# Perceiver block on one core: key and value tiles interleaved, the attention loop's side work in another order

## The reference

```python
x = x + xattn(layernorm(x), ctx, ctx)   # 32 query heads, 8 key and value heads, head size 128, rope, causal
x = x + attn(layernorm(x))              # 32 heads of size 16, biases, causal
x = x + ffn(layernorm(x))               # base product + 8 experts of rank 16, gated by softmax - threshold
```

## Time and profile before

| | |
|---|---|
| profiled execution, its time | 786.1 us |
| its span, first to last instruction | 784.3 us |
| median of three runs | 786.59 us |
| PE busy | 724.8 us (92%) |
| DVE, ACT, POOL busy | 522.3, 376.0, 495.8 us |
| mean granted TensorE clock | 0.983 of full speed |
| DMA | 51.09 MB, mean 65 GB/s |
| chain that ended last | PE 55%, DVE 14%, POOL 12%, issue 11%, ACT 4% |

### The profile page before, as it was taken

The page is one execution under the profiler, slowest core; times in us unless marked ns, Lnnn a source line. Parts: engine busy times, 40 slices in busy tenths (PEclk is TensorE's granted clock), DMA queues, the critical chain, the costliest instruction groups (busy, mean ns, idle before and its releaser), DMA issues.

```text
span 784.3 us, 12899 instructions
## 1 busy us (share of the span) xinstructions
PE 724.8 (92%) x4848; PEld 566.7 (72%) x4848; DVE 522.3 (67%) x826; ACT 376.0 (48%) x555; POOL 495.8 (63%) x371
## 2 busy tenths in 40 slices
PE   8979995789999999999999999996999999999898
PEld 6758884667776786776777777775787777777786
DVE  4663545875676766846947847746567878888855
ACT  5455535535454444544643743543235676664220
POOL 4995307856677678676866866846323798975350
PEclk9999999989999999999999999997999999999999
DMA  8343461031121211302201201201100110011002
GB/s 330 108 161 122 121 187 54 1 122 38 58 68 41 81 39 40 107 13 66 81 29 51 94 27 54 95 3 60 48 0 1 42 39 18 1 36 48 14 1 107
DMA packets 25561, 51.09 MB, mean 65 GB/s; under 512 B 2352, under 2 KB 10672, under 8 KB 25520
## 3 DMA queue, kind: packets, MB, share of 16 engines
q1 hardware_dynamic: 25520, 50.53, 19.2%
HBM read 40.04 MB, written 10.49 MB: 64 GB/s over the span
## 4 chain that ended last, share of the span: by engine, by line
PE 55%; DVE 14%; POOL 12%; issue 11%; ACT 4%; DMA 2%; SPq 0%; DVEq 0%; POOLq 0%; ACTq 0%
PE pj L1594 7%; PE pj L1500 7%; PE pj L1413 7%; PE sc L1500 6%; PE pv L1399 6%; PE tp L1413 5%; POOL sw L464 4%; PE pv L1487 3%; POOL qr L470 2%; PE sc L1641 2%; PE tp L1500 2%; DVE cq L1009 2%; PE tp L1654 2%; PE pv L1665 2%; POOL sm L470 2%
## 5 line engine op out<-in xcount | busy, mean ns | idle before, releaser
L464 POOL TENSOR_TENSOR sw<-sw,cst 128x512 f32<-128x512 f32 x80 | 115.3, 1441 | 92.1 <-ACT sw L618 92.1
L488 POOL TENSOR_TENSOR sm<-sm,mx 128x512 f32<-128x512 f32 x64 | 73.6, 1151 | 71.9 <-DVE mx L1080 36.0
L1413 PE MATMUL pj<-x,w 128*128 128x512 f32 x384 | 103.5, 406 | 14.7 <-DVE cq L1009 13.4
L1413 PEld LDWEIGHTS pj<-x,w 128*128 128x128 f32 x384 | 70.0, 190 | 37.2 <-DVE cq L1009 17.5
L470 POOL TENSOR_TENSOR qr<-t,sw 128x512 f32<-128x512 f32 x64 | 86.0, 1344 | 9.2
L717 ACT ACTIVATE sm<-sm 128x512 f32<-128x512 f32 x64 | 40.4, 632 | 104.9 <-POOL sm L488 104.9
L493 POOL TENSOR_TENSOR sm<-sm,rz 128x512 f32<-128x512 f32 x64 | 72.2, 1132 | 15.7 <-DVE rz L1095 15.6
L482 POOL TENSOR_TENSOR w<-raw,w 128x896 fp32r<-128x896 f32 x28 | 58.7, 2119 | 24.5 <-ACT w L598 24.5
L1413 PE MATMUL tp<-x,w 128*128 128x512 f32 x270 | 72.1, 403 | 0.0
L1594 PE MATMUL pj<-xh,ws 128*128 128x512 f32 x192 | 66.3, 405 | 0.2 <-ACT kb L797 0.2
L1099 DVE TENSOR_TENSOR cl<-pv,ch 128x1024 fp32r<-128x1024 f32 x32 | 39.0, 1220 | 29.4 <-ACT ch L725 29.4
(11 more groups left out here) (252 smaller groups left out, 1798.7 us busy)
## 6 DMA issues: line engine op xcount, KB each, us to landing
rawd<-in_w_d SPq DMA_DIRECT2D x16, 512.0 KB, 3.3
raw<-in_w_q SPq DMA_DIRECT2D x15, 512.0 KB, 3.3
kscr<-sm SPq DMA_DIRECT2D x16, 256.0 KB, 2.1
vscr<-sm SPq DMA_DIRECT2D x16, 256.0 KB, 2.3
kr<-kscr SPq DMA_DIRECT2D x8, 512.0 KB, 3.3
vv<-vscr SPq DMA_DIRECT2D x16, 256.0 KB, 2.6
raw<-in_w_k SPq DMA_DIRECT2D x4, 512.0 KB, 6.5
cT<-in_ctxT SPq DMA_DIRECT2D x4, 512.0 KB, 6.5
```

Source lines behind the costliest of these rows:

```text
L464: pool.tensor_tensor(bs(sw[par][:, :]), bs(sw[par][:, :]), rep(cst[:, C_SIN:C_SIN + S], HB), ALU.mult).then_inc(sin_done, 1)
L488: pool.tensor_tensor(s3, s3, per_group(mx[:, c, :], 8), ALU.subtract).then_inc(subbed, 1)
L1413: last = pe.matmul(bank, a, r, start=(start and k == 0 and part == 0), stop=(stop and k == 1 and part == 2), skip_group_check=True)
```

## The change

- PHASE1 puts one value tile in front of each two key tiles from the fifth key tile on; the weights' pieces come in the order Wk, Wk, Wv, Wv, Wk, Wk, Wv, Wv. The first piece's lo part moves from POOL to DVE, the second's stays on POOL; pieces 2 and 3 are loaded, rounded and split earlier. Key tile 0 runs its hi·hi matmuls first, then lo·hi, then hi·lo. The layer norm's transposes follow value tiles 4 to 7.
- First group: the weights' sums of the fourth pair come two `c_add` later; the rope additions 5 and 7 are on DVE; the split of the third pair (on DVE) comes after the last cosine; that of the fourth goes from DVE to POOL.
- Head: the second half of `wd_split` goes behind `c_lo`; the sums of softmax (`sum_rec`) of chunks 2 and 3 come later; `w7_sum` of the second pair comes earlier; ACT rounds the second pair's weights before the swaps, and does `c_hi` between the last two swaps; POOL splits the first pair's weights before the second pair's ropes.
- Last head: `late_hi` and `late_lo` come after the softmax, and ACT copies the first transposed chunk before the third exponential.

```diff
...
+PHASE1 = [("k", i) for i in range(4)] + [(t, i) for v in range(6) for t, i in
+                                         (("v", v), ("k", 4 + 2 * v), ("k", 5 + 2 * v))] + \
+         [("v", i) for i in range(6, NVT)]
...
         kst, vst = sm4[0:2], sm4[2:4]
+        pieces = [wk[0][:, :, :, :], wk[1][:, :, :, :], wv0[:, :, 0:2, :], wv0[:, :, 2:4, :],
+                  wk[0][:, :, :, :], wk[1][:, :, :, :], wv1[:, :, 0:2, :], wv1[:, :, 2:4, :]]
+        piece_src = [w_k[0], w_k[1], w_v[0], w_v[1], w_k[2], w_k[3], w_v[2], w_v[3]]
         raw2 = [raw8[:, 4 * i:4 * i + 4, :].rearrange("p n c -> p (n c)") for i in range(2)]
...
             load_ctx(0, 1)
-            sp.dma_start(cst[:, :], consts).then_inc(s_const, 16)
             load_piece(1)
...
             load_ctx(1, 1)
+            sp.dma_start(cst[:, :], consts).then_inc(s_const, 16)
+            sp.wait_ge(plo_d, 1)
+            load_piece(2)
+            sp.wait_ge(plo_p, 1)
+            load_piece(3)
             for i in range(4):
                 load_x(i)
-            load_piece(2)
-            load_piece(3)
             sp.dma_start(bcol[:, :, :], bias_cols).then_inc(s_cols, 16)
...
                 spill_k(ki)
-                if ki in (4, 6, 8, 10):
-                    load_piece(4 + (ki - 4) // 2)
-                if ki == 14:
-                    sp.wait_ge(plo_d, 6)
+                if ki in (1, 2, 6, 8):
+                    j = {1: 4, 2: 5, 6: 6, 8: 7}[ki]
+                    sp.wait_ge(plo_d, j - 2)
+                    load_piece(j)
+                if ki == 12:
+                    sp.wait_ge(plo_d, 7)
                     load_q(0, 0)
-            for vi in range(NVT):
-                if vi == 5:
+                if ki % 2 == 0 and 2 <= ki <= 12:
+                    spill_v(ki // 2 - 1)
+            for vi in range(6, NVT):
+                spill_v(vi)
+                if vi == 8:
                     sp.wait_ge(wlo, 2)
                     load_q(0, 1)
-                elif vi == 11:
+                elif vi == 13:
                     sp.wait_ge(wlo, 4)
-                    load_q(1, 0)
-                spill_v(vi)
+                    load_q(1, 1)
...
             pool.wait_ge(mh_set, 1)
-            wk_lo(0)
-            wk_lo(1)
+            piece_lo(1)
             pool.wait_ge(s_const, 16)
...
                 rope_k(ki)
-                if ki in (5, 9):
-                    ln_pow((ki - 5) // 4)
+                if ki in (5, 7):
+                    ln_pow((ki - 5) // 2)
             for m in range(2):
...
                 rope_sin(i % 2, Q0 + i)
-                rope_add(i % 2, Q0 + i, q_out(p, k))
-
-            def head(g, n, more):
+                if i not in FIRST_DVE:
+                    if i - 1 in FIRST_DVE:
+                        pool.wait_ge(rope, Q0 + i)
+                    rope_add(i % 2, Q0 + i, q_out(p, k))
+            def head(g, n, more, first=False):
                 for c in range(2):
...
                         rope_add(k % 2, ri(2 * n + p, k), q_out(p, k))
-                        if p == 0 and k == 1:
-                            for c in range(2, 4):
-                                normalise(4 * g + c, c)
-                        if p == 1 and k in (0, 3) and more:
-                            w7_lo(2 * n + 2 + k // 3, k // 3)
-
-            head(0, 1, True)
+                        if first and p == 0 and k == 0:
+                            w7_lo(3, 1)
+                    if p == 0:
+                        for c in range(2, 4):
+                            normalise(4 * g + c, c)
+                    if more:
+                        w7_lo(2 * n + 2 + p, p)
+            head(0, 1, True, True)
             with pool.Fori(1, NKV - 2) as g:
...
             q = 4 * (NKV - 1)
-            late_lo(0)
             subtract_max(q, 0)
...
             subtract_max(q + 3, 3)
-            late_lo(1)
             normalise(q + 2, 2)
             normalise(q + 3, 3)
+            late_lo(0)
+            late_lo(1)
             late_lo(2)
...
-            for ki in range(NKT):
-                if ki == 5:
-                    act.wait_ge(kproj, 6)
-                    piece_hi(2)
-                elif ki == 8:
-                    act.wait_ge(kproj, 8)
-                    piece_hi(3)
-                elif ki in (9, 11, 13, 15):
-                    piece_hi(4 + (ki - 9) // 2)
-                swap_k(ki)
-                if ki >= 12:
-                    ln_copy(ki - 12)
-            for vi in range(NVT):
-                v_copy(vi)
-                if vi < 4:
-                    ln_copy(4 + vi)
-                elif vi < 8:
-                    block_hi(vi - 4)
-                elif vi == 9:
-                    block_hi(4)
-                if vi == 2:
+            for t, i in PHASE1:
+                if t == "k":
+                    if i == 6:
+                        act.wait_ge(kproj, 6)
+                        piece_hi(4)
+                    elif i == 8:
+                        act.wait_ge(kproj, 8)
+                        piece_hi(5)
+                    elif i in (9, 11):
+                        piece_hi((i + 3) // 2)
+                    swap_k(i)
+                    if i in (1, 2):
+                        piece_hi(i + 1)
+                    continue
+                v_copy(i)
+                if 4 <= i < 8:
+                    ln_copy(2 * i - 8)
+                    ln_copy(2 * i - 7)
+                if i == 6:
                     act.wait_ge(kproj, NKT)
...
                 wdhi(g, 1, wdh)
-                if first:
-                    w7_hi(3, 1, 14, raw8b)
                 part_copy(u2, 14 * n + 3, A_BANK)
...
                 exp(q + 3, 3, X_SCALE)
+                if first:
+                    w7_hi(3, 1, 14)
                 c_hi(q, 0)
...
                 p_copy(q + 3, 3)
-                turn(1, 2)
-                turn(1, 3)
-                c_hi(q + 3, 3)
                 if more:
                     w7_hi(2 * n + 3, 1, 14 * n + 14)
+                turn(1, 2)
+                c_hi(q + 3, 3)
+                turn(1, 3)
...
             act.wait_ge(stp, 7 * N_PAIR)
-            late_hi(0)
             wdhi(g, 0, wd7h)
...
             exp(q + 1, 1, X_SCALE)
+            p_copy(q, 0)
+            c_hi(q, 0)
+            exp(q + 2, 2, X_SCALE)
+            p_copy(q + 1, 1)
+            exp(q + 3, 3, X_SCALE)
+            late_hi(0)
             late_hi(1)
-            exp(q + 2, 2, X_SCALE)
-            p_copy(q, 0)
-            exp(q + 3, 3, X_SCALE)
-            c_hi(q, 0)
...
+            def rope_add(i):
+                p, k = FIRST[i]
+                dve.wait_ge(t1_done, Q0 + i + 1)
+                dve.wait_ge(sin_done, Q0 + i + 1)
+                dve.wait_ge(rope, Q0 + i)
+                dve.tensor_tensor(q_out(p, k), bs(t1[i % 2][:, :]), bs(sw[i % 2][:, :]), ALU.add).then_inc(rope, 1)
...
+            piece_lo(0)
             ctx_lo(0, range(KT))
...
                 t1_k(ki)
-                if ki in (2, 4):
-                    stats_half(ki // 2 - 1)
-                elif ki == 5:
-                    piece_lo(2)
-                elif ki in (8, 9, 11, 13, 15):
-                    piece_lo({8: 3, 9: 4, 11: 5, 13: 6, 15: 7}[ki])
-                if ki in (10, 11, 13, 14):
-                    ln_apply({10: 0, 11: 1, 13: 2, 14: 3}[ki])
-            ln_apply(4)
-            ln_apply(5)
+                if ki in (3, 5):
+                    stats_half((ki - 3) // 2)
+                elif ki in (1, 2, 6, 8, 9, 11):
+                    piece_lo({1: 2, 2: 3, 6: 4, 8: 5, 9: 6, 11: 7}[ki])
+                if ki in (11, 13):
+                    ln_apply(ki - 11)
+                    ln_apply(ki - 10)
+            for n in range(4, NT):
+                ln_apply(n)
             w7_sum(0)
-            ln_apply(6)
-            ln_apply(7)
...
                 t1_mul(p, Q0 + 2 + p, cq[p][:, :])
+            w7_sum(3, raw8b)
             for p, a in enumerate((A_BANK, A2)):
...
                 t1_mul(p, Q0 + 4 + p, a)
-            for p, (c, copy) in enumerate(((C_BANK, u2), (C2, u2b))):
-                c_add(p, 13 + p, 6, Q0 + 3 + p, c, copy)
-                dve.wait_ge(cadd, 5 + p)
-                t1_mul(p, Q0 + 6 + p, cq[p][:, :])
-                if p == 0:
-                    w7_lo(2, 0, raw8)
+            c_add(0, 13, 6, Q0 + 3, C_BANK, u2)
+            dve.wait_ge(cadd, 5)
+            t1_mul(0, Q0 + 6, cq[0][:, :])
+            rope_add(5)
+            c_add(1, 14, 6, Q0 + 4, C2, u2b)
+            dve.wait_ge(cadd, 6)
+            t1_mul(1, Q0 + 7, cq[1][:, :])
+            w7_lo(2, 0, raw8b)
+            rope_add(7)
             for i in range(2):
...
                 if first:
-                    w7_lo(3, 1, raw8b)
-                    dve.wait_ge(wlo, 8)
+                    dve.wait_ge(wlo, 6)
                 wd_split(g, 0, wdh, wdl)
-                wd_split(g, 1, wdh, wdl)
                 c_mix(0, 1)
...
                 c_lo(q, 0)
```

(44 more changed lines are left out.)

66 lines of the change are left out of this document (28 added, 38 removed).

## The result

| | before | after |
|---|---|---|
| median of 18 executions each, us | 787.61 (785.83 to 788.84) | 779.59 (774.73 to 786.31) |
| ratio after / before | | 0.9897 [0.9875, 0.9919] |
| profiled execution, us | 786.10 | 775.39 |
| its span, us; mean granted clock | 784.3; 0.983 | 773.6; 0.982 |

The change makes the kernel 8.0 us (1.0%) faster. The prediction was 764.3, with a range from 753 to 774: the direction is right, the size is not, and the time lies outside the range. Two things stand in the table. The profiled execution gained 10.7 us, not 22; and the executions after the change lie 11.6 us apart, where those of before lie 3.0 apart, so that the median is 4.2 us above the profiled one.

What follows compares the result with a forecast made beforehand. PE was taken as the bound, busy 95% of the loop, leaving its waits and low clock to win. Terms of 1.9, 7.5, 10.2 and 2.4 took 22.0 us off 786.1: 764.1, stated as 764.3, range 753 to 774.

Steps and rivals of the forecast that it cites:

- Term 1: First phase: interleaved ropes end old waits, one new 6.3 us wait comes at value tile 0; phase ends at 108.1, −1.9 us.
- its worst end was +1: First phase, worst case: each DVE step blocked by a POOL step of 1.3, value tile 0 at 28; +1 us.
- Term 2, first group: First group: later weights' sums and a DVE rope addition start PE's scores at 135.6 instead of 137.54, −1.9 us.
- Term 2, head 0: Head 0: the fourth weights' split leaves DVE and one wd_split moves back, ending the 4.56 us wait; −5.6 us.
- its lower end: First group and head 0, worst case: POOL's split blocks DVE's work and is late for its product; −4 us.
- Term 3: Loop: the 1.14 us waits mostly go and the 1.38 us waits shrink to 0.3, less 1.8 lost; −10.2 us.
- Rival B: First phase gives nothing, loop only its first wait, as c_hi behind two more ACT steps delays PE; 773, 20%.
- C: Slower: POOL becomes the bound of the loop, with weight split and last swap delaying its additions; 790, 4%.
- Term 4: Last head: scores some 2 us later, pv_x 0 3.1 earlier, less low clock, pv_x 2 held 2.9; −2.4 us.
- four rivals: Better than the sum 754, 20%; loop's first wait only 773, 20%; POOL-bound loop 790, 4%; costlier value tile 0 771, 4%.
- signs of being right: About 6 us idle near 19 to 25, phase end near 108, scores near 134, pass 54.1, out_x 6 wait 0.3.
- signs of being wrong: Value tile 0 starting at 20 or 30, a pass of 55.5 or more, scores waiting for POOL's additions in each head.

Runs made afterwards that it cites:

- e7_sum1_early: Changed kernel with DVE forming the sums of weight group 1 right after the first two block differences, as in the kernel before: 772.7 us, ratio 0.9811.
- e1_copy_first: Changed kernel with ACT rounding the high part of weight group 1 after the copy of value tile 12 instead of ahead of it: 778.6 us, ratio 0.9888.
- e4_loop_only: Kernel before with only the new loop body and last head; first phase, first group and head 0's split of the fourth weights as before: 776.3 us, ratio 0.9859.
- e8_last_head: Changed kernel with head 6's last swap ahead of the last high part and the third late high part behind the copy PE waits for: 771.8 us, 0.9778.
- e2_sum_back: Changed kernel with the sums of the fourth weights back ahead of the second two rope additions on DVE: 776.4 us, ratio 0.9868.

## Why the prediction was wrong

**Term 1 (−1.9, measured +4.45): the wrong step.** Its own numbers held: value tile 0 started at 26.06 (25.2 predicted) after a wait of 6.20 (6.3), at the low clock. It failed at "After that 28 tiles and 8 transposes", which took the rest of the phase as PE's own work, from "none of those waits should come back". That looked at ropes alone and did not walk the lists of DVE and ACT through the end of the phase, where the diff had moved the sums of group 1 behind five more steps. The missing items are 3.44 us of wait and 1.7 of half clock behind it (the two tiles took 7.14 us, their share at full clock is 5.44). In the six profiles that have this first phase unchanged it ends at 114.2 to 115.2. Nor did its range hold them: its worst end was +1. `e7_sum1_early` took both away and gave 5 to 6 us; `e1_copy_first` showed that ACT's queue is only where it surfaces. The rest of the 6.3 us between 108.1 and 114.38 is value tile 0, 0.9 later than predicted, and 1.4 us of waits at the layer norm where 1.0 was taken.

**Term 2, first group (−1.9, measured +1.40).** Right up to POOL's third rope. It failed at "The fifth addition on DVE takes 1.3 off POOL's chain" and at leaving the moved sums free: they went from a place where POOL waited to one where it worked, at 1.5 instead of 0.42 us a step, 4.2 us more, and held ropes 4 and 5. The rule on the shared interface that the prediction cited from the Trainium skill ("SBUF — State Buffer", "Who interferes with whom") was weighed for two steps of the first phase and for the rope additions, and not for these four, where the trace shows it at its dearest. Undoing either move alone changed the time by less than can be told.

**Term 2, head 0 (−5.6, measured −4.69).** The product came 17.4 us after the first scores (18.3 predicted), so the wait of 4.56 went as forecast. What was missed is named in its lower end: POOL's split (5.18 us in the trace, 4.2 taken) held DVE's next multiplication for 3.55 us, and PE waited 2.75 us at 180 where 0.5 was charged. The two parts of term 2 together measured −3.29, just outside its worst end of −4.

**Term 3 (−10.2).** Right in both waits and in size, if anything too small: the five passes of heads 1 to 5 took 268.6 us instead of 278.8, 10.2 off without the sixth; 53.70 us a pass against 54.1, the 1.38 us waits at 0.26 (0.3 predicted), the 1.14 us waits gone. `e4_loop_only` shows it without the rest of the change. Rival B, which held that ACT would keep PE waiting there, is out, and so is C: POOL did not become the bound of the loop.

**Term 4 (−2.4).** Right in kind: the scores wait 3.05 us (2 predicted) for the last swap, `pv_x` 2 2.95 us (2.9). From the last head's scores on 3.55 us came off, of which 2.8 had been lost just ahead of them, so the term is −0.7. The 1.7 us that are missing come from that wait, which grew by 2.8 where 2 were taken, and from the low clock behind it: the 64 scores took 3.58 us, where the same took 2.08 before. The two make 2.3; 0.6 was made good elsewhere. `e8_last_head` shows that both waits were there to be had for nothing. The last head's scores in the changed kernel:

```profile
524.00 3.58 PE L1490 MATMUL sc<-kr,qr 128*64 128x64 f32 x64 [3.05 <-POOL qr L480]
```

**The rivals and signs.** None of the four rivals has a first phase that gets slower, and the 779.6 us lie outside all of them. Of the signs of being right, the 6 us at value tile 0, the pass and `out_x` 6 came true; "no long wait to 105" failed with the wait that ends at 107.24, the phase ended at 114.38 instead of 108, and the first scores came at 143.39 instead of 134. None of the signs of being wrong that were named appeared.

**The step from the profile to the median.** The prediction put the median 0.2 us above the sum on the profiled execution; it was 4.2 above, where the kernel before has 1.5. Waits of 3 us were charged at their length; they also cost 1.2 to 1.6 us of half clock in some executions and not in others, which is the likely reason, though only two executions of the changed kernel were profiled. These 4 us are about a quarter of the 15 by which the number was off. The range failed because its ends were added up from terms that had no item for a wait that no row of before shows.

## What to carry to other kernels

When a change reorders several in-order queues, walk each moved step's own engine to the end of the stage, and for each step name what stands behind it on that engine and who waits for that; a weight chain that passes through DVE, ACT, POOL and a load is as long as its latest link, and shifting the place where it surfaces gains nothing. Place two-input DVE steps where POOL is quiet: their price depends on the neighbour more than on their size. Treat a wait of about 3 us of PE as two costs, its length and a clock that may be at half behind it, here 1.2 to 1.6 us. And compare a stage over more than one profile before giving it a price of 1 to 3 us.

## What the runs showed of the hardware that was not expected

A DVE subtraction or addition of 128x256 with both inputs in SBUF took 0.42 us alone and 1.37 to 1.52 beside POOL's rope steps of 1.3 us or more, four in a row each ending 0.3 us after a POOL step; in `e2_sum_back` the first of the four took 1.43 us beside such a step and the other three 0.41 when POOL had none. So each short step waited for a POOL step, and four of them lose more than one long one (128x1024: 1.22 alone, 1.62 to 1.98 beside such steps). And PE's clock behind waits of 2.75 to 3.44 us was at 2.4 GHz in some executions and at 1.2 GHz in others of kernels that are the same up to there; behind the 6.2 us at value tile 0 it was at 1.2 GHz in all ten profiles that have that wait (two matmuls in 1.22 us, against 0.62).
